# A graph network layer on one core: the tail block of each graph moved inside chunk 3, setup steps re-ordered, and the first groups' moments and the last group's power moved on POOL

## The reference, cut to what matters

```python
def layer0(h, adj):                       # h = relu(layernorm(x))
    mask = (adj > 0.0)
    xj = h @ W1a
    diff = h[:, :, None, :] - h[:, None, :, :]
    e = relu(xj[:, :, None, :] + diff @ W1b + b1)      # H = 192
    hm = einsum('bjkh,bjk->bjh', e, mask)
    return hm @ W2 + sum(mask, -1)[..., None] * b2
def layer1(h, adj):                       # h = relu(layernorm(x))
    return einsum('bnm,bmf->bnf', adj, h) @ W.T
x = x + layer0(relu(layernorm(x)), adj)
x = x + layer1(relu(layernorm(x)), adj)
```

## Time and profile before

| what | us |
|---|---|
| median of 3 runs | 842.6 |
| lowest and highest | 842.23, 845.79 |
| the profiled execution | 845.98 |
| its span, first to last instruction | 844.1 |
| PE, DVE busy | 810.6, 809.9 |
| ACT, POOL busy | 794.9, 611.5 |
| span up to the first `consume` of graph 0 | 56.9 |

### The profile page before, as it was taken

How to read it: one execution, slowest core, us unless ns; L and a number is a source line. 1 busy time by engine, 2 the same in 40 slices (tenths; PEclk the granted TensorE clock), 3 DMA queues, 4 the chain that set the end, 5 groups by cost and what they waited for, 6 DMA issues and landing times.

```text
span 844.1 us, 26648 instructions
## 1 busy us (share of the span) xinstructions
PE 810.6 (96%) x8242; PEld 715.0 (85%) x8243; DVE 809.9 (96%) x2894; ACT 794.9 (94%) x2246; POOL 611.5 (72%) x1174
## 2 busy tenths in 40 slices
PE   4879999999999999999999999999999999999996
PEld 2447888898889888988998899888988898889884
DVE  6969999999999999999999999999999999999993
ACT  4969999999999999999999999999999999999992
POOL 1966777777777777777777777777777777777762
PEclk8979999999999999999999999999999999999996
DMA  9800000000000000000000000000000000000000
GB/s 337 327 1 2 7 9 21 21 21 15 21 20 21 9 21 21 20 15 21 21 21 9 20 21 21 15 21 20 21 9 21 21 20 14 21 21 21 15 3 21
DMA packets 26705, 27.55 MB, mean 33 GB/s; under 512 B 3520, under 2 KB 24512, under 8 KB 25536
## 3 DMA queue, kind: packets, MB, share of 16 engines
q1 hardware_dynamic: 25488, 25.37, 8.9%
q10 hardware_dynamic: 1072, 0.43, 0.2%
HBM read 21.59 MB, written 4.19 MB: 31 GB/s over the span
## 4 chain that ended last, share of the span: by engine, by line
PE 90%; DVE 4%; issue 2%; ACT 2%; DMA 1%; SPq 0%; ACTq 0%; DVEq 0%
PE ring L414 48%; PE ring L442 8%; PE prep L471 5%; PE post L514 4%; PE post L501 3%; PE post L508 3%; PE post L502 3%; PE prep L479 3%; PE prep L482 2%; PE prep L477 2%; DVE acc L826 2%; PE post L506 2%; DMA x_all<-x_nbf_dram 1%; PE prep L473 1%; DVE onehot_space L812 1%
## 5 line engine op out<-in xcount | busy, mean ns | idle before, releaser
L826 DVE SCALAR_TENSOR_TENSOR acc<-ring,acc 128x384 f32<-128x384 f32 x896 | 488.6, 545 | 0.6
L572 ACT COPY ring<-P 128x384 f32<-128x384 f32 x1024 | 466.6, 509 | 19.3 <-DVE acc L826 11.4
L414 PE MATMUL ring<-PQ,onehot_space 128*128 128x192 f16 x4096 | 417.0, 247 | 4.5 <-ACT ring L572 2.2
L414 PEld LDWEIGHTS ring<-PQ,onehot_space 128*128 128x128 f16 x4096 | 328.0, 99 | 39.4 <-issue 13.5
L922 POOL TENSOR_SCALAR start<-P,spare 128x192 f32<-128x192 f32 x128 | 128.4, 1003 | 134.8 <-ACT P L622 133.8
L946 POOL TENSOR_TENSOR row_space<-row_space 128x192 f32<-128x192 f32 x256 | 153.4, 599 | 25.3 <-ACT row_space L610 8.2
L812 DVE TENSOR_SCALAR onehot_space<-mask_all 128x512 f16<-128x512 f16 x512 | 158.1, 311 | 0.0
L442 PE MATMUL ring<-PQ,owner 128*128 128x384 f16 (+1 forms) x512 | 93.9, 306 | 0.0
L414 PE MATMUL ring<-PQ,onehot_row 128*128 128x192 f16 x768 | 84.3, 246 | 0.5 <-DVE onehot_row L874 0.3
L610 ACT ACTIVATE row_space<-ring 128x576 f32<-128x576 f32 x128 | 83.3, 651 | 0.7 <-PE ring L414 0.7
L826 DVE SCALAR_TENSOR_TENSOR acc<-ring,start 128x384 f32<-128x384 f32 x128 | 71.1, 556 | 5.3 <-PE ring L414 1.3
(11 more groups left out here) (138 smaller groups left out, 1431.9 us busy)
## 6 DMA issues: line engine op xcount, KB each, us to landing
onehot_space<-adj_kbj_dram SPq DMA_DIRECT2D x8, 1024.0 KB, 17.3
adj_again<-adj_kbj_dram SPq DMA_DIRECT2D x128, 64.0 KB, 2.0
x_all<-x_nbf_dram SPq DMA_DIRECT2D x8, 512.0 KB, 19.0
out_dram<-x_all SPq DMA_DIRECT2D x32, 128.0 KB, 1.9
consts<-consts_dram SPq DMA_DIRECT2D x1, 192.0 KB, 2.4
scratch<-w1a_dram ACTq DMA_DIRECT2D x2, 48.0 KB, 4.2
scratch<-w1b_dram ACTq DMA_DIRECT2D x2, 48.0 KB, 6.7
scratch<-b_dram ACTq DMA_DIRECT2D x1, 96.0 KB, 10.1
```

Of the source, the lines that this page charges most:

```text
L414: last = nc.tensor.matmul(to, hot(s), parts[:, part, H:2 * H], start=False, stop=(part == 1), skip_group_check=True)
L572: return nc.scalar.copy(slots[to][:, bank_], src.unsqueeze(1).broadcast_to([N, PER_BANK, H]))
L826: return nc.vector.scalar_tensor_tensor(sums, slots[to][:, bank_], 0.0, start[:, :, :] if first else sums, ALU.max, ALU.subtract if first ...
```

## The change

Line numbers of the changed kernel differ; names are the same. The parts:

- SP issues adjacency's part g and behind it x's part g - 1, for all g; the store of the last four graphs becomes two of two graphs.
- PE: the codes of parts 0 to 2 stand ahead of the first scale product, those of part 3 between the two. The block at the end of chunk 3 is now the function `across`, called behind bank 0 of chunk 3 and so ahead of bank 1, and in it the wait for `hm_row_ready` stands behind the two transposes of L501. The first four banks of the ring are written ahead of the table sums.
- ACT: the copy of ownerT goes from behind that of code_row to behind the third of the four seeds of chunks 2 and 3; DVE waits for the copy of code_row by a semaphore of its own. The wait for the tables ahead of the main loop goes. In the drain both graphs' second norm are taken together (`second_norm`).
- DVE: masks and statistics of the setup in another order, without the moments of groups 0 and 1; the one-hots of chunk 0 and two of chunk 1 stand ahead of the tables. In step 128 DVE adds up the last rows.
- POOL: it makes the moments of groups 0 and 1 in eight operations each, ahead of each power. The last group's 32-column power, until now ahead of graph 0, becomes four of 8 columns behind POOL's work in steps 3, 5, 7 and 9.

The diff, cut to its core:

```diff
                     sp.wait_ge(mask_ready, g - STAGES + 1)
                 sp.dma_start(adj_stage[g % STAGES], adjT[:, g * PER_PART:(g + 1) * PER_PART, :]).then_inc(adj_in[g], 16)
-                if g < EARLY:
-                    x_part(g)
-                elif g > EARLY:
+                if g > 0:
                     x_part(g - 1)
...
-            sp.wait_ge(y_ready, B // 2)
-            sp.dma_start(out[:, B - STORE:B, :], x_all[:, B - STORE:B, :]).then_inc(stored, 16)
-            sp.wait_ge(stored, 16 * B // STORE)
+            for done in range(B - STORE + 2, B + 1, 2):
+                sp.wait_ge(y_ready, done // 2)
+                sp.dma_start(out[:, done - 2:done, :], x_all[:, done - 2:done, :]).then_inc(stored, 16)
+            sp.wait_ge(stored, 16 * (B // STORE - 1 + STORE // 2))
...
             codes(0)
-            codes(1, range(QUADS // 2))
+            codes(1)
+            codes(2)
...
-            codes(1, range(QUADS // 2, QUADS))
+            codes(3)
...
-            with pe.Fori(2, LATE) as g:
+            with pe.Fori(EARLY, LATE) as g:
...
+            def across(b, u, looped, t):
+
+                main = exists(b)
+                last = None
+                if main:
+                    pe.wait_ge(rows_ready, b + 1)
+                if exists(b + 2):
...
+                if exists(b - 1):
...
+                    for s in range(PER_BANK):
+                        nc.tensor.matmul(head_ps, acc_space[:, (u - 1) // 2 % 2, s, heads[(u - 1) % 2]], ident, start=(s == 0), stop=False, is_transpose=True)
+                    pe.wait_ge(hm_row_ready, b)
+                    last = nc.tensor.matmul(head_ps, row_heads[(u - 1) % 2], ownerT[:, (u - 1) % QUAD, :], start=False, stop=True)
...
                                 gather(dst, parts, hot).then_inc(gathered, 1)
+                                if i == 3 and bank_ == 0:
+                                    across(b, u, looped, t)
...
-                    if i == 3:
...
+                    if i == 3 and not main:
+                        across(b, u, looped, t)
...
-            pe.wait_ge(rows_counted, 1)
-            nc.tensor.matmul(tables[:, 0, :], ones[:, :], rows, start=True, stop=True)
-            nc.tensor.matmul(tables[:, 1, :], rows, ones[:, :], start=True, stop=True).then_inc(rows_summed, 1)
...
             pe.wait_ge(code_kj_ready, B // QUAD)
-            pe.wait_ge(code_jk_ready, B // QUAD)
-            write_ring(range(QUADS))
+            write_ring(range(QUADS)).then_inc(ring_ready, 1)
+
+            pe.wait_ge(rows_counted, 1)
+            nc.tensor.matmul(tables[:, 0, :], ones[:, :], rows, start=True, stop=True)
+            nc.tensor.matmul(tables[:, 1, :], rows, ones[:, :], start=True, stop=True).then_inc(rows_summed, 1)
...
+                if exists(b - 9):
+                    act.wait_ge(transposed, transposes(b - 2 if u % 2 else b - 3))
+                k = (u - 5) // 2 % 2
+                for g in range(2) if not exists(b - 1) else ((u - 5) % 2,):
+                    of = b - 5 - (u - 5) % 2 + g
+                    nc.scalar.activation(h2[:, k, 2 * g, :], x_all[:, of, :], ACT.Relu, bias=shift2[:, k, g:g + 1],
+                                         scale=rstd2[:, k, g:g + 1]).then_inc(h2_ready, 1)
...
+                        if i == 2 and isinstance(b, int) and b == 0:
+                            act.wait_ge(ring_ready, 2)
...
                             seed(place(u, i), P[:, u % 2, :], bank_).then_inc(seeded, 1)
+                            if i == 3 and bank_ == 0:
+                                nc.scalar.copy(ownerT[:, u % QUAD, :], ownerT_ps).then_inc(rows_ready, 1)
...
+                    if i == 0 and isinstance(b, int) and b == B + 4:
+                        second_norm(b - 1, u - 1, t)
...
-                        nc.scalar.copy(code_row[:, :], code_row_ps)
-                        nc.scalar.copy(ownerT[:, u % QUAD, :], ownerT_ps).then_inc(rows_ready, 1)
+                        nc.scalar.copy(code_row[:, :], code_row_ps).then_inc(code_row_ready, 1)
...
+                    if i == 4 and exists(b - 5) and (u % 2 or exists(b - 1)) and not (isinstance(b, int) and b == B + 3):
+                        second_norm(b, u, t)
...
+                        if isinstance(b, int) and b == BODY - 1:
+                            act.wait_ge(norm1_ready, GROUPS - 1 + PIECES)
...
             codes(0)
-            codes(1)
-            codes(2)
+            with nc.scalar.Fori(1, EARLY) as g:
+                codes(g)
+            codes(EARLY)
+            act.wait_ge(norm1_ready, 1)
+            lead(step, hi=-1)
             act.wait_ge(scale_ready, 1)
             nc.scalar.activation(w_parts[:, 0, :, 0:H], w_pq[:, :].rearrange("p (k h) -> p k h", k=3), ACT.Copy,
                                  scale=to_scale[:, 2:3]).then_inc(first_parts_ready, 1)
-            codes(3)
-            act.wait_ge(norm1_ready, 1)
-            lead(step, hi=-1)
-            with nc.scalar.Fori(EARLY, PARTS) as g:
+            with nc.scalar.Fori(EARLY + 1, PARTS) as g:
                 codes(g)
             lead(step, lo=-1)
...
-            act.wait_ge(tables_ready, 1)
             act.wait_ge(ring_ready, 1)
...
+                for s in range(SLOTS):
+                    last = hot(0, 0, 0, s)
+                last.then_inc(onehot_ready, 1)
+
             mask(0)
+            mask(1)
             norm1_stats(0)
-            mask(1)
-            norm1_stats(1)
             largest()
             mask(2)
+            norm1_stats(1)
+            mask(3)
+            norm1_stats(2)
+            mask(4)
             largest_of_rows()
-            moments(0)
-            norm1_stats(2)
+            norm1_stats(3)
+            mask(5)
             scale()
-            mask(3)
-            norm1_stats(3)
-            moments(1)
-            mask(4)
-            second_parts()
-            mask(5)
             norm1_stats(4)
             mask(6)
             norm1_stats(5)
+            second_parts()
+            mask(7)
             moments(2)
-            mask(7)
             norm1_stats(6)
             norm1_stats(7)
             moments(3)
+            dve.wait_ge(code_kj_ready, 1)
+            first_hot()
 
...
             chain(nc.vector.tensor_copy(deg[:, :], edges_i))
 
-            dve.wait_ge(p_ready, 1)
-            second_part(0, 0)
-
+            hot(0, 0, 1, 0)
+            hot(0, 0, 1, 1)
             dve.wait_ge(rows_summed, 1)
...
             dve.wait_ge(owned_sums, 1)
             nc.vector.tensor_scalar(loops[0:1, 0, :], tables[0:1, 3, :], float(LOOPED), None, ALU.mult)
-            nc.vector.tensor_copy(row_count[:, :], owned)
             chain(nc.vector.tensor_tensor(first_row[:, :], tables[:, 2, :], owned, ALU.subtract))
             nc.vector.tensor_scalar(first_code[:, :], first_row[:, :], 2.0 * ROW_SLOTS, None, ALU.mult).then_inc(tables_ready, 1)
...
                 at = bass.ds(b + 1, 1)
+                if not main and b == B:
+
+                    dve.wait_ge(relu_row_ready, B)
+                    sums = relu_rows[(u - 1) % 2][:, 0, :]
+                    nc.vector.tensor_tensor(sums, sums, relu_rows[(u - 1) % 2][:, 1, :], ALU.add).then_inc(half_row_ready, 1)
+                    dve.wait_ge(half_row_ready, B)
+                    nc.vector.tensor_tensor(sums, sums, relu_rows[(u - 1) % 2][:, 2, :], ALU.add).then_inc(hm_row_ready, 1)
                 for i in range(CHUNKS):
                     if i == 3 and main and exists(b + 1):
...
 
-            for s in range(SLOTS):
-                last = hot(0, 0, 0, s)
-            last.then_inc(onehot_ready, 1)
             lead(step)
             graphs(nc.vector, step, load_any(nc.vector))
...
+
+            m_even, m_odd, s_even, s_odd = (stats1[:, :, k] for k in (1, 4, 2, 5))
+
+            def moments(k):
+
+                pool.wait_ge(stats1_ready, k + 1)
+                b = slice(k * GROUP * PER_PART, (k + 1) * GROUP * PER_PART)
+                nc.gpsimd.tensor_tensor(mom[:, 0, b], m_even[:, b], m_odd[:, b], ALU.add).then_inc(mean_ready, 1)
+                nc.gpsimd.tensor_tensor(mom[:, 1, b], m_even[:, b], m_odd[:, b], ALU.subtract).then_inc(gap_ready, 1)
...
+                pool.wait_ge(gap_ready, 3 * k + 1)
+                nc.gpsimd.tensor_tensor(mom[:, 3, b], mom[:, 1, b], mom[:, 1, b], ALU.mult).then_inc(gap_ready, 1)
+                pool.wait_ge(spread_ready, 2 * k + 1)
+                nc.gpsimd.tensor_scalar(mom[:, 2, b], mom[:, 2, b], 1.0 / F**3, EPS / F**2, ALU.mult, ALU.add).then_inc(spread_ready, 1)
...
+                nc.gpsimd.tensor_tensor(mom[:, 3, b], mom[:, 3, b], mom[:, 2, b], ALU.add).then_inc(moments_ready, 1)
+
+            def last_norm1(k):
+
+                piece = GROUP * PER_PART // PIECES
+                b = slice(B - (PIECES - k) * piece, B - (PIECES - k - 1) * piece)
+                pool.wait_ge(moments_ready, GROUPS)
```

(19 more changed lines are left out.)

108 lines of the change are left out of this document (55 added, 53 removed).

## The result

The changed kernel takes **847.8 us** (median; 847.29 to 849.13), the kernel before beside it 843.6 (842.23 to 845.79). The ratio is 1.0049 with a 95% interval of 1.0035 to 1.0063: **4.1 us slower** where 3.6 less was forecast. The profiled execution of after has a span of 847.2 us, 3.1 more than that of before.

A forecast was written before the change was run, and what follows sets the result against it. The prediction took a four-graph chain of waits through PE, DVE and ACT to bound the main loop. Its terms, -5.0 + 4.4 - 1.9 - 1.1 = -3.6 us, took the median from 842.6 to 839.0 us, range 833 to 844.5.

The forecast's parts named there:

- Main loop, -5.0: Main loop: moving the block and ownerT's copy saves 0.16 us per four-graph turn, 31 turns, 5.0 us saved.
- This loop is the bound of the main part: Main loop: a chain of waits through PE, DVE and ACT takes 24.0 us for four graphs, 6.0 each.
- Rival 4: Main loop: the one-hot's hold by POOL grows by what PE gains; 5.0 us less saved, 844.0 us; chance 0.13.
- Pieces, +4.4: Main loop: four 8-column power pieces on POOL stall PE 1.1 us each, 4.4 us lost.
- hidden now behind graph 0: Ahead of graph 0: the last group's 32-column power, 5.54 us on POOL, was taken as hidden.
- Setup, -1.9: Setup: codes end 1.4 us earlier, and the tables and ready one-hots gain more; 1.9 us saved in sum.
- 0.3 gained: Setup: with the bank writes ahead of the table sums, DVE's L804 comes at 50.9 instead of 51.19.
- the 1.6 of the one-hots: Setup: six of thirteen one-hots are already made while DVE waits for codes or PE; 1.6 us gained.
- Port: Main loop: by the rows, not the skill page's exclusion rule, the pieces' power costs DVE nothing directly.
- Drain, -1.1: Drain: DVE adds the last row sums, so L502 starts at 828.7 instead of 829.85; 1.1 us saved (0.5 to 1.3).
- Median from the profiled execution: Whole kernel: the median of timed runs, 842.6 us, lies 3.4 below the profiled execution; the forecast starts from that median.
- Sum: Whole kernel: -5.0 + 4.4 - 1.9 - 1.1 = -3.6 us, giving a median of 839.0 us.

The follow-up runs named there:

- b_block: Kernel before with the main-loop edit alone (block behind bank 0 of chunk 3, ownerT copied behind the third seed, own semaphore for code_row): 842.5 us, ratio 0.9980.
- a_pad2: Changed kernel with two more DVE instructions ahead of the first mask: 844.2 us, ratio 1.0004; on another chip 844.25 us, ratio 1.0014.
- n_tables_first: Changed kernel without pieces, last codes ahead of the scaling wait, two more DVE instructions, table sums ahead of bank writes: 840.4 us, ratio 0.9977.
- shift 0, 4 or 16: Changed kernel with no (1.0049) or four (1.0009) more DVE instructions before the first mask, or moments on DVE, 16 places on (1.0016).
- shift 1, 2 or 3: Changed kernel with one, two or three more DVE instructions ahead of the first mask: ratios 1.0051, 1.0004 (again 1.0014) and 1.0059.
- a_pad4: Changed kernel with four more DVE instructions ahead of the first mask: 845.0 us, ratio 1.0009.

## Why the prediction was wrong, step by step

- **Main loop, -5.0: wrong, the step that failed.** "This loop is the bound of the main part" was read from one turn: the late fourth seed, PE without a gap, DVE without a gap. Over graphs 12 to 124 the edit gained nothing in any pair in which late sums play no part: +0.7, 0.0 and +2.2 us, each to within 2. The runs show two things in its place. In b_block the seed of the even graph came as late as before (0.30 of 0.27), while POOL's add held the one-hot twice as often and DVE had hardly any idle time left (0.7 of 690 us). In a_pad2 neither happened, and PE stood 9.0 us for POOL's row sums instead: the loop of the earlier trace rows was not alone, and others through DVE and POOL were as long. What the edit did bring, 0.8 to 1.3 us in the first twelve graphs and something behind the last, the sum had left out. Rival 4 named the hold and its place and had 0.13; no rival named the wait for POOL's row sums. The size should have warned: between 130 and 820 us DVE was idle for 4.4 us of 690 in all, PE for 2.1, and the forecast took 5.0.
- **Pieces, +4.4: right in mechanism and near in size.** 8 columns take 1.66 us (forecast 1.7), the piece 1.93 (1.95), graphs 4 to 12 take 4.0 more. PE's stall was 0.83, for 1.1 forecast. Mis-sized was "hidden now behind graph 0": the 32-column power cost 1.1 there, so the pieces' net price is 2.9.
- **Setup, -1.9: wrong, it was 0** (graph 0 at 56.5 and 56.0, before 56.2). The scaling of w2 ended at 41.6, not 40.2. The sum let POOL start on the second moments with their statistics, at 26.6; POOL was on the first group's power until 28.3, started the second moments at 28.59 and the second power at 30.89, not 28.7. Part of that is the first moments, eight operations in 3.3 us and not 2.1, one of them 1.34 beside a DVE mask. The codes ended at 47.05 instead of 44.9. The second failed term is "0.3 gained" for the banks ahead of the sums: the sums came 2.8 us behind the counts instead of 1.1, which took the 1.6 of the one-hots. That the second term matters for the total is not shown: with the sums ahead of the banks again (n_tables_first) the kernel gained 0.4.
- **Port.** As forecast from the earlier trace rows, the pieces' power held no DVE instruction for its length; the adds did.
- **Drain, -1.1: right**, 1.7 measured with an interval of 0.9 to 2.5; PE's gap fell by the 1.1 forecast.
- **Median from the profiled execution.** I took the profiled execution's 3.4 us above the median off evenly. If they belonged to its drain, as the clock there suggests, its stages up to graph 127 were typical and its end was not. That didn't move the forecast, but it made the traces look as if the drain had gained 3.9.
- **Sum.** 0 (setup) + 2.9 (pieces) - 1.7 (drain) - 0.9 (edit in the first graphs) and +1.8 to +3.9 between graphs 12 and 124: 2.1 to 4.2 by the stages, against 4.1 (2.9 to 5.3) by the ratio. The last term is the one that no single edit explains; the traces put it in the stretch where the same kernel differs by up to 2 us between executions. The same main loop took from 673.6 to 678.4 us there in the kernels that differ from the changed one only ahead of graph 12.

## What to carry to other kernels

When three engines are busy all the time, a wait on the path is no proof that its removal pays: compare the forecast gain with the idle time that the full engines have at all, and look which other wait takes its place, here a one-hot that another engine's add holds, or that engine's sums themselves. Long work put between two steps of a queue reaches whoever waits behind it: of a piece's 1.93 us about 1.0 came through to the time of graphs 4 to 12. An effect under 1% on a loop that repeats 128 times has to be tried with the same code shifted by a few instructions: here two more instructions made one kernel 3.8 us faster, one 6.2 faster and two about 2 slower, as much as most edits.

## What the runs showed of the hardware

- On DVE, an instruction that is number 63 modulo 128 starts 0.35 us late where it stands just behind a wait for PE (in every kernel with shift 0, 4 or 16, in the graphs where a first sum falls on such a place, and in none with shift 1, 2 or 3); DVE shows no idle time ahead of the other 25 such places in the loop of after. The profile shows instruction code arriving in transfers of 8 KB on a queue of its own (76 transfers, 0.62 MB). One of them starts within 0.3 us before and 1.0 us behind each of the 29 instructions of DVE that are number 63 modulo 128 in that loop, and within 0.5 and 1.0 us in before, a_pad2, a_pad4 and n_tables_first; from places 31 or 95 modulo 128 the nearest is up to 9 us off. So the places go with the arrival of DVE's code. Why the instruction starts late there is argued, not shown.

```profile
q14 instruction: 76, 0.62, 0.2%
```

- The Trainium skill (page "Runtime: NRT & Kernel Launch", section "Instruction fetch mechanics") has blocks of 256 instructions and calls the cost of crossing one mostly hidden. Here the places repeat every 128 instructions, and the cost is hidden at most of them, but not at every one.
- The same kernel before had medians of 842.3 to 844.5 us on five chips, so only kernels run on one chip, or their ratios, were compared.
